# Edge products ahead of the message sums in the last four groups, and one gathered tile moved from GpSimd to TensorE, in a graph attention kernel

## What is computed

```python
Qh = (x @ Wq.T + bq).reshape(n, H, D)
Kh = (x @ Wk.T + bk).reshape(n, H, D)
Vh = (x @ Wv.T + bv).reshape(n, H, D)
Ee = (edge_attr @ We.T + be).reshape(-1, H, D)
score = (Kh[src] * Qh[dst] * (1.0 / np.sqrt(D)) * Ee).sum(-1)
score = jnp.exp(jnp.clip(score, -5.0, 5.0))
msg = Vh[src] * score[..., None]
wV = jax.ops.segment_sum(msg, dst, num_segments=n)
out = _layernorm(x + wV.reshape(n, H * D), axis=-1)
```

## Time and profile before

| | |
|---|---|
| median of three executions | 1672.18 us (1670.16 to 1672.41) |
| the profiled execution | 1674.01 us, span 1671.8 us |
| PE busy | 1574.8 us, 94% |
| DVE busy | 1439.3 us, 86% |
| POOL busy | 1220.7 us, 73%, in 1266 gathers for the most part |
| ACT busy | 944.4 us, 56% |
| mean granted clock of TensorE | 0.975 of full speed |

### The profile page before, as it was taken

One profiled execution on the slowest core, in us unless ns is written; L12 is line 12 of the kernel. 1 busy time (PEld: TensorE's weight loads), 2 busy tenths in 40 slices (PEclk: granted clock), 3 DMA queues, 4 the chain that ended last, 5 costly groups with the idle time before them and its releaser, 6 DMA issues. The chain is left out here.

```text
span 1671.8 us, 57996 instructions
## 1 busy us (share of the span) xinstructions
PE 1574.8 (94%) x18014; PEld 1394.3 (83%) x18014; DVE 1439.3 (86%) x2549; ACT 944.4 (56%) x2857; POOL 1220.7 (73%) x1298
## 2 busy tenths in 40 slices
PE   5399999999999999999999999999999999999994
PEld 5288888888888888888888888888888888888884
DVE  7389888889889889889889889889889889889886
ACT  3355555555555555555555555555555556556553
POOL 5577777777777777777777777777777777777772
PEclk9599999999999999999999999999999999999995
DMA  9455555555555555555555455555555555455541
GB/s 286 145 141 138 144 140 137 143 141 137 138 145 139 135 146 141 135 145 141 135 144 143 135 141 146 134 139 147 136 136 150 136 135 150 135 137 149 135 126 50
DMA packets 197529, 236.34 MB, mean 141 GB/s; under 512 B 95865, under 2 KB 122593, under 8 KB 197313
## 3 DMA queue, kind: packets, MB, share of 16 engines
q1 hardware_dynamic: 156992, 152.99, 32.7%
q0 software_dynamic: 40512, 83.05, 20.5%
HBM read 228.46 MB, written 7.40 MB: 141 GB/s over the span
## 5 line engine op out<-in xcount | busy, mean ns | idle before, releaser
L283 POOL DMA_INDIRECT kv<-kv_table,idx x1266 | 1203.4, 951 | 410.5 <-issue 388.5
L689 PE MATMUL xg_bank<-x_hi,src_onehot 128*128 128x448 f32 x2422 | 903.3, 373 | 16.7 <-DVE src_onehot L827 10.4
L690 PE MATMUL xg_bank<-x_lo,src_onehot 128*128 128x448 f32 x2422 | 883.6, 365 | 0.0
L689 PEld LDWEIGHTS xg_bank<-x_hi,src_onehot 128*128 128x128 f32 x2422 | 454.9, 188 | 77.0 <-issue 15.3
L690 PEld LDWEIGHTS xg_bank<-x_lo,src_onehot 128*128 128x128 f32 x2422 | 455.4, 188 | 33.2
L766 ACT ACTIVATE distance<-iota_w,dst_neg 128x64 f32<-128x64 f32 x1612 | 428.7, 340 | 0.0
L827 DVE TENSOR_TENSOR src_onehot<-r_row,xg_bank 128x896 fp32r<-128x896 f32 x346 | 372.8, 1077 | 16.0 <-DMA r_row<-r_table 16.0
L839 DVE SCALAR_TENSOR_TENSOR x_sel<-iota_v,src_block,xg_bank 128x448 f32<-128x448 f32 x346 | 233.8, 676 | 23.9 <-PE xg_bank L690 20.2
L792 ACT COPY xg_t_sb<-turn_sum 128x128 f32<-128x128 f32 x198 | 53.0, 268 | 349.1 <-PE turn_sum L699 349.1
L845 DVE TENSOR_REDUCE xg_sb<-x_sel 128x64 f32<-128x448 f32 x346 | 214.4, 620 | 11.9
L871 DVE TENSOR_TENSOR kq<-kv,edge_ps 128x512 f32<-128x512 f32 x202 | 138.2, 684 | 95.3 <-ACT kv L799 92.3
(11 more groups left out here) (111 smaller groups left out, 904.4 us busy)
## 6 DMA issues: line engine op xcount, KB each, us to landing
attr_sb<-attr SPq DMA_DIRECT2D x201, 256.0 KB
dst_row<-dst_rows SPq DMA_DIRECT2D x402, 128.0 KB
kv<-kv_table,idx POOLq DMA_INDIRECT x1266
r_row<-r_table SPq DMA_DIRECT2D x148, 128.0 KB
q_win<-q_table SPq DMA_DIRECT2D x404, 24.0 KB
idx<-src_tab SPq DMA_DIRECT2D x206, 4.0 KB, 4.3
r_row<-r_table SPq DMA_DIRECT2D x50, 64.0 KB
kv_table<-kv_stage SPq DMA_DIRECT2D x7, 448.0 KB, 4.2
```

The lines of the kernel that those rows point to most:

```text
L283: pool.indirect_dma_start(out=kv[:, slot, t, :], out_offset=None, in_=kv_table, in_offset=bass.IndirectOffsetOnAxis(ap=idx[:, slot, t:t + ...
L689: pe.matmul(xg, src_onehot[:, parity, u, :], x_hi[:, u, :], start=(u == 0), stop=False)
L690: mm = pe.matmul(xg, src_onehot[:, parity, u, :], x_lo[:, u, :], start=False, stop=(u == U - 1))
```

## The change

From step 198 on, PE makes edge products, queries and projection of group g + 1 first and the message sum of g - 1 after them. A wait for the message of g - 1 stands ahead of the edge products in its stead. Group 200 gets one tile of TensorE, so POOL gathers 7 tiles of it and not 8. `Q`, the number of TensorE's tiles, goes from 346 to 347, and the tables of source rows and columns hold one tile more.

```diff
+EDGES_FIRST = PE_END - 2
-Q = PE_EACH * ITERS - PE_SKIPPED
+Q = PE_EACH * ITERS - PE_SKIPPED + 1
...
         def pe_tiles(g, slot):
-            return 0 if isinstance(g, int) and not PE_FROM <= g < PE_END else PE_OF[slot]
+            if isinstance(g, int) and not PE_FROM <= g < PE_END:
+                return 1 if g == PE_END else 0
+            return PE_OF[slot]
...
                         if turned:
                             turn_x(g + 1, i, j + 1)
-                        if not (isinstance(g, int) and g == 0):
+                        edges_first = isinstance(g, int) and g >= EDGES_FIRST
+                        if not edges_first and not (isinstance(g, int) and g == 0):
                             sum_messages(g - 1, (j - 1) % SLOTS)
+                        if edges_first:
+                            pe.wait_ge(msg_made, g)
                         if not last:
                             multiply_edges(g + 1, i + (j + 1) // SLOTS, (j + 1) % SLOTS)
                             fetch_q(g + 1, i + (j + 1) // SLOTS, (j + 1) % SLOTS)
                         if turned:
                             project(g + 1, j + 1)
+                        if edges_first:
+                            sum_messages(g - 1, (j - 1) % SLOTS)
...
-    pe_src[:Q] = np.concatenate([src_tiles[g, T - PE_OF[g % SLOTS]:] for g in range(PE_FROM, PE_END)])
+    pe_src[:Q] = np.concatenate([src_tiles[g, T - PE_OF[g % SLOTS]:] for g in range(PE_FROM, PE_END)] + [src_tiles[PE_END, T - 1:]])
```

## The result

The changed kernel takes **1667.9 us**, the median of 9 executions (1665.55 to 1669.03); the kernel before takes 1670.57 us in 9 (1669.39 to 1673.03). The ratio is 0.9979, with a 95% interval of 0.9969 to 0.9989: 3.5 us less (1.8 to 5.2); the medians alone are 2.7 us apart. The forecast was 1668.2 us and 0.9976.

The account below looks back on a forecast made before the run. The last 40 us were taken as bound by PE and DVE waiting for each other, with PE at half clock. Kq gains of 1.94, 3.35 and 4.0 us are cumulative: 1672.18 - 4.0 = 1668.2 us, range 1666.6 to 1671.3.

Parts of the forecast that it names:

- The bound: Last 40 us of the edge pass: PE and DVE wait for each other; the start of kq of group 201 counts.
- One-hot of group 200 at no price: DVE, step 197: its 1.08 us fit into DVE's idle time ahead of kq of group 198; price zero.
- 14 matmuls: PE, step 198, group 200's tile: start near 1629.85, take 2.83 us up to the turn of group 199.
- Full clock, and kq of 199 1.94 us earlier: Step 198: PE without a gap stays at 2.4 GHz; kq of group 199 at 1635.15, not 1637.09.
- kq of 200 3.35 us earlier: Step 199: kq of group 200 at 1639.6, not 1642.94, waiting for ACT's copies and distances behind the exponential.
- kq of 201 4.0 us earlier: Kq of group 201 at 1643.6, not 1647.63, its queries ready before DVE asks for them.
- The chain behind kq of 201: From kq of group 201 a chain through DVE to the last sum, then layer norm; taken to move unchanged.
- The sum: Whole change: -4.0 us, from 1672.18 to 1668.2 us, 0.24% less.
- the second case of the prediction: Rival, chance 0.27: in other executions the kernel before has a better end, so the gain is only 2.1 us, 1670.1.
- The price of the tile: Group 200's tile on PE costs 0.8 us at kq of group 200; ACT and DVE tie at group 199.
- the clock did not fall at 1632: Rival, chance 0.13: PE's clock falls at 1632.0 although PE works on; gain only 1.0 us, 1671.2.
- DVE didn't wait for source rows: Sign that would show the forecast wrong: DVE waiting for group 200's source rows, which had 11 us to land.

Follow-up runs that it names:

- order-only: Edge products first from step 198 as in the change, but group 200 stays with POOL, no moved tile: 1665.98 us, 0.9969 of the kernel before.
- clock-held: Kernel before in its old order, plus seven unread matmuls on PE ahead of the message sum in steps 198, 199 and 200: 1667.94 us, ratio 0.9975.

## Why the prediction was right, point by point

- *The bound.* The end was 30.53 us from kq of 197 in the profile that the prediction had, and is 25.66 now. The loop kept its pace: from the kq near 95 us to that of group 197 it took 1526.16 us, against 1526.34 and 1526.11 in the two profiles of before.
- *One-hot of group 200 at no price.* Right; it ran in DVE's gap, and kq of 198 stayed 8.32 us behind that of 197.
- *14 matmuls.* 2.94 us from the first to the turn, 2.83 predicted; the first one starts slower, 0.31 us before the second.
- *Full clock, and kq of 199 1.94 us earlier.* 4.83 us behind kq of 198 and so 1.93 us earlier. ACT's copy and DVE's select do end together.
- *kq of 200 3.35 us earlier.* By the intervals 3.54; ACT's copy came 0.96 us behind the start of the distances, and not 1.06, and the following steps were 0.1 us shorter. The chain (exponential, turned copy, four distances, projected copy) is the one that was told, and PE's projection is idle 1.24 us for it, off the path.
- *kq of 201 4.0 us earlier.* 4.38: 1647.63 - 1642.51 less the 0.74 us of the loop.
- *The chain behind kq of 201.* The prediction let it move unchanged, and this was the wrong step, a small one. It shortened by 0.49 us, 4.91 to 4.42. Before, the even sum stood 0.81 us behind the start of kq of 201, with 0.39 us of it without a releaser; after, it stands 0.33 us behind, at 1642.84. In the order-only profile, where kq of 201 doesn't wait either, it is 0.34 us. In the first profile of before it reads:

```profile
1648.44 0.21 DVE L854 TENSOR_TENSOR acc<-acc,turn_sum 64x64 f32 x1 [0.39 <-issue]
```

  My reading is that the address of that sum is loaded on DVE's own queue and that this load is hidden only when DVE isn't waiting. It is not shown: no run took the load away, and in the clock-held kernel kq of 201 doesn't wait and the sum still stands 0.60 us behind it, with 0.20 us idle.
- *The sum.* -4.0 us was predicted, -4.87 is what the two profiles show for the end: 0.38 us more at kq of 201 and 0.49 us behind it. The timed runs show 3.5, 4.2 and 4.5 us by their ratios. Between trace and timing stands, as far as known, **the second case of the prediction**, to which it gave 0.27: the kernel before has a better end in some executions. That end was shown directly, 2.34 us better. The prediction had 1.9: 1.91 came at kq of 199, and 0.43 more at kq of 200, which it hadn't counted. With 10 such executions in 52 the mean gain would be, by estimate, 4.87 - 10 / 52 x 2.34 = 4.4 us. In the first comparison 5 of the 9 times of before lie below 1670.7 us, and the same estimate gives 3.6. The prediction listed the case as a rival of the forecast; in fact both hold, by the execution, as its own sentence on the gain between the two numbers has it. Its rule from the Trainium skill (TensorE: Matmul & The Clock Gate, Part 1), that the moment of the clock's change varies from run to run, holds in the two profiles of before: near 1632.0 in one and between 1635 and 1636 in the other, with the same gap ahead.
- *What was luck.* The forecast of 1668.2 us is 0.3 us from the measured median, closer than its parts are. It starts from 1672.18, the median of three executions, where nine give 1670.57; the end in the profiles shortened by 0.9 us more than it said, and the medians fell by 1.3 us less. The order of the kqs and what released them came by its reasoning, the last 0.3 us didn't.
- *The price of the tile.* The prediction said 0.8 us at group 200 and a tie at group 199. Order only against the full change: 0.51 at 199, 0.67 at 200, 0.23 at 201, 1.40 us in all and 1.56 us in time on one chip. By the medians on that chip order only is 6.1 us below before, so of the change's two edits one gains and the other gives a quarter of it back.

The cases that didn't come: the clock did not fall at 1632, DVE didn't wait for source rows, the loop kept its pace.

What the change would have been worth without the clock is not one number. In the old order it takes 30.5, 28.2 or 26.0 us by the clock's fall; in the new order without the tile the end is bound by DVE, and 24.26 us came out with a fall right behind the gap. That fall costs nothing there. Against the clock-held end of 26.0 us the order gives 1.7 us, and the rest of its gain, 2.2 or 4.5 us by the profile of before, is the clock's: the larger part of what the order does. For the changed kernel itself, with the tile, an early fall wasn't seen in a profile.

## What to carry to other kernels

Where PE runs dry at the end of a long pass, its clock may fall in the first gap, at a moment that differs between executions, and what follows runs at half speed; one profile shows one draw of it, so take a second one before sizing such an end. Work that another engine waits for should go ahead of work that waits for that engine, and here this also left nothing for the clock to cost (24.26 us for the end, against 26.00 with the gaps filled by matmuls). A tile moved from an engine whose last work was issued 12 us before anyone needed it gained nothing, and cost 1.4 us in the queues of the other engines that it passes.

## What the runs showed that was not expected

21 matmuls whose result nobody reads made the kernel 0.25% faster (0.9964 to 0.9985). The kernel before has two kinds of executions on one core, 1668.7 to 1670.7 and 1670.8 to 1674.4 us, whose mean granted clocks don't overlap; part of the difference lies in the first 95 us and part in the end. The 1526 us of loop between them agree within 0.3 us in all profiles but that of the slow chip. That chip ran both kernels in some 2970 us, with a mean clock of 0.758 in the profile; why isn't known.
